# SyncE waits for the first maximum row of the second quad before it issues the next image's query copies

## What is computed

```python
h = group_norm(x, groups=32) * gamma + beta
q, k, v = split(einsum('oc,bct->bot', qkv_w, h) + qkv_b)      # per head, 16 channels
w = softmax(einsum('bct,bcs->bts', q * s, k * s))             # 1024 x 1024 per head, s = 16 ** -0.25
a = einsum('bts,bcs->bct', w, v)
x = x + einsum('oc,bct->bot', proj_w, a) + proj_b
```

## Time and profile before

| | us |
|---|---|
| median of 3 runs | 2296.9 |
| lowest and highest run | 2295.36, 2297.52 |
| span of the profiled execution | 2295.6 |
| PE busy | 2201.2 (96%) |
| DVE busy | 1815.8 (79%) |
| ACT busy | 1719.9 (75%) |
| eight-head part, up to | about 1714 |

### The profile page before, as it was taken

The page is one execution under the profiler, slowest core; times in us unless marked ns, Lnnn a source line. Parts: engine busy times, 40 slices in busy tenths (PEclk is TensorE's granted clock), DMA queues, the critical chain, the costliest instruction groups (busy, mean ns, idle before and its releaser), DMA issues. The chain is left out here.

```text
span 2295.6 us, 34006 instructions
## 1 busy us (share of the span) xinstructions
PE 2201.2 (96%) x11776; PEld 972.2 (42%) x11776; DVE 1815.8 (79%) x3176; ACT 1719.9 (75%) x3107; POOL 520.6 (23%) x689
## 2 busy tenths in 40 slices
PE   3999999999999999999999999999989999999998
PEld 1223232323333232333333232333326888888887
DVE  2878888888888878888888888888837777777776
ACT  1467677777877777776767777776777888888887
POOL 3113030202213030311203020211113333333331
PEclk9999999999999999999999999999999999999999
DMA  6053351606244261616345160615112112121111
GB/s 82 7 70 53 58 78 35 104 22 91 41 69 66 45 90 36 95 27 84 50 61 76 36 103 22 94 37 75 26 31 72 53 48 66 36 65 57 42 53 49
DMA packets 81647, 132.31 MB, mean 58 GB/s; under 512 B 17632, under 2 KB 50528, under 8 KB 81504
## 3 DMA queue, kind: packets, MB, share of 16 engines
q1 hardware_dynamic: 78240, 129.70, 32.5%
q10 hardware_dynamic: 3264, 0.79, 0.2%
HBM read 53.12 MB, written 17.83 MB: 31 GB/s over the span
## 5 line engine op out<-in xcount | busy, mean ns | idle before, releaser
L447 DVE TENSOR_REDUCE h_half_nmax<-h_s_ps 128x1 f32<-128x512 f32 x2048 | 1285.8, 684 | 270.2 <-PE h_s_ps L682 263.0
L598 ACT ACTIVATE h_probs<-h_st_ps 128x512 f32<-128x512 f32 x2048 | 1103.7, 600 | 388.2 <-PE h_st_ps L819 382.2
L682 PE MATMUL h_s_ps<-h_krep,h_qrep 96*128 96x512 bf16 x2048 | 795.7, 389 | 22.4 <-SPq L232 20.8
L819 PE MATMUL h_st_ps<-h_qrep,h_krep 99*128 99x512 bf16 x2048 | 779.9, 382 | 35.1 <-DMA h_qrep<-h_mrow 24.3
L674 PE MATMUL h_pv<-h_probs,h_vT 128*32 128x512 f32 x4096 | 548.1, 607 | 0.9 <-ACT h_probs L598 0.7
L682 PEld LDWEIGHTS h_s_ps<-h_krep,h_qrep 96*128 96x128 bf16 x2048 | 200.0, 98 | 677.3 <-DVE h_half_nmax L447 503.0
L819 PEld LDWEIGHTS h_st_ps<-h_qrep,h_krep 99*128 99x128 bf16 x2048 | 201.7, 99 | 230.6 <-DMA h_qrep<-h_mrow 36.4
L347 POOL TENSOR_SCALAR h_nparts<-h_nmax 128x16 bf16<-128x16 f32 x64 | 16.4, 256 | 956.6 <-DVE h_nmax L455 956.6
L1334 PE MATMUL o_s<-o_k,o_q 128*128 128x512 f32 x768 | 225.7, 430 | 7.4 <-DVE o_q L1155 5.8
L1334 PE MATMUL o_pv<-o_pT,o_vT 128*128 128x512 f32 x768 | 208.1, 406 | 0.8 <-ACTq L1261 0.8
L1149 DVE TENSOR_TENSOR o_pT<-o_t,o_pT 128x512 fp32r<-128x512 f32 x256 | 164.5, 684 | 43.8 <-ACT o_pT L1286 41.4
(11 more groups left out here) (116 smaller groups left out, 1380.1 us busy)
## 6 DMA issues: line engine op xcount, KB each, us to landing
h_krep<-h_kp SPq DMA_DIRECT2D x96, 256.0 KB, 8.7
h_qrep<-h_qp SPq DMA_DIRECT2D x192, 128.0 KB, 9.5
x_res<-out_dram SPq DMA_DIRECT2D x24, 512.0 KB, 3.7
num<-av SPq DMA_DIRECT2D x128, 64.0 KB
rrep<-rden_dram SPq DMA_DIRECT2D x16, 512.0 KB
out_dram<-o_y SPq DMA_DIRECT2D x16, 512.0 KB
out_dram<-h_y SPq DMA_DIRECT2D x15, 512.0 KB, 2.6
o_x_in<-out_dram SPq DMA_DIRECT2D x15, 512.0 KB, 3.5
```

The costliest lines, as they stand in the source:

```text
L447: reduce = nc.vector.tensor_reduce(half_nmax[:, c, unit:unit + 1], s_ps[bank(2 * n + c)][:, :], AX.X, ALU.max, negate=True)
L598: nc.scalar.activation(probs[g % 2][:, j, :], st_ps[bank(n)][:, :], ACT.Exp, scale=1.0 / CH ** 0.5).then_inc(exp_done, 1)
L682: nc.tensor.matmul(s_ps[bank(n)][:, :], qrep[par][0:KS, th, head, tile * P:(tile + 1) * P], krep[par][0:KS, head, c * HALF:(c + 1) * HALF] ...
L819: nc.tensor.matmul(st_ps[bank(n)][:, :], krep[par][0:KM, head, st * P:(st + 1) * P], qrep[par][0:KM, th, head, :], start=True, stop=True). ...
```

## The change

`replicate` gets a third argument, `rows`. Where it is given, SP waits, after the query parts are ready and before the query copies, until `mrow_dma` has counted that many rows. In the body it is given as `4 * u + 3`: the third row of that image's count, which is the one of the second quad's first half. The copies at the start of the program pass nothing. No DMA is added or removed, and PE's program is unchanged.

```diff
-            def replicate(par, u):
+            def replicate(par, u, rows=None):
 
                 sp.wait_ge(parts_ready, 2 * u + 1)
                 for term, part in enumerate((0, 1, 2, 0, 1, 0)):
                     sp.dma_start(krep[par][term * CH:(term + 1) * CH, :, :], parts["k"][:, part, :]).then_inc(rep_dma, 16)
                 sp.wait_ge(parts_ready, 2 * u + 2)
+                if rows is not None:
+                    sp.wait_ge(mrow_dma, 16 * rows)
                 for term, part in enumerate((0, 0, 0, 1, 1, 2)):
                     for th in range(2):
                         sp.dma_start(qrep[par][term * CH:(term + 1) * CH, th, :, :],
...
                     if not (last and u == 1):
-                        replicate(1 - u, u)
+                        replicate(1 - u, u, 4 * u + 3)
```

## The result

The changed kernel takes 2267.9 us (median of 4 runs, 2266.39 to 2268.76) beside 2297.2 for the kernel before on the same chip: ratio 0.9875, 95% interval 0.9862 to 0.9887, 29.3 us faster. The forecast was 2279.5, from 2269 to 2291. The profiled span fell from 2295.6 to 2265.9.

A forecast was written before the change was run, and what follows sets the result against it. PE was taken as the bound, held up by a row standing behind query copies. Gain 31.0 less 13.6 of new waits is 17.4 us; span 2295.6 becomes 2278.2, with the median 1.3 above: 2279.5, range 2269 to 2291.

The forecast's parts named there:

- What the row's lateness cost, 31.0: PE's waits on the maximum row at quad hand-overs, with lowered clock behind two: 31.0 us, all gained by the change.
- m: The start of the maximum row's DMA issue by ACT, from which the prediction counts times in us.
- SP's start, m + 2.4: SP, after waiting for the row's landing, issues the query copies from about m + 2.4; bounds 1.9 and 3.3.
- The copies, 16.9 from issue to matmul: Query copies: first bytes 1.3, transfer 14.1 at 111 GB/s, landing to PE's matmul 1.5; sum 16.9 us.
- The new wait, 0.8 an image: PE waits 0.8 us for the query copies in each of 14 ordinary images, 11.2 us together.
- The first image, 2.4: Without output projections, PE wants the first image's copies at m + 16.94 and waits 2.4 us; no clock loss counted.
- SP's later work, free: Store of y, four loads and gather, queued on SP behind the copies, start later but cost nothing; cover 5.0 us.
- the copies land in time: Rival: copies need 16.1 us or less, so ordinary images have no new wait; 30.9 us gained, 2266.0, chance 0.12.

The follow-up runs named there:

- the run with the first copies alone: Changed kernel, but at the program's start SP waits for the six key copies to land before issuing the twelve query copies; 2270.5 us, one run.
- the thirteenth copy: Changed kernel plus one 128 KB copy to a spare buffer behind the twelve query copies, waited for with them; 2285.1 us, ratio 0.9942.
- the delay: Changed kernel plus a 12 KB DMA issued and waited for between the row's landing and the query copies, some 2.3 us; 2325.8 us, ratio 1.0123.
- the run that waits for the keys: Changed kernel, but SP waits for the landing of the six key copies instead of for the row; 2285.6 us, ratio 0.9952.

## Why the forecast missed, step by step

- **What the row's lateness cost, 31.0: held.** The waits on the row are gone, L821 starts at m + 6.83, and neither hand-over loses the clock. Counted from the rows, 31.0 less what is left of new waits (1.9, below) is 29.1; the spans differ by 29.7. The last transposed score tile of the eight-head layers moved from 1713.4 to 1684.9, 28.5; the rest of the 29.7 lies in the one-head layers, which the change doesn't touch. Counted image by image in the trace before, the first row score comes 30.8 us later in sum than it does with six copies ahead; the first image's part of that is 5.5, where the prediction had 2.89 + 2.88.
- **SP's start, m + 2.4: m + 2.28.** Within the bounds, 0.1 off.
- **The copies, 16.9 from issue to matmul: 16.1. This is the step that failed.** Its parts: first bytes 1.2 for 1.3, bytes 13.4 for 14.1, landing and wake-up some 1.5 as taken. The 14.1 came from 111 GB/s, read where query copies run behind keys; on empty queues they move at 117 on the mean, which the run with the first copies alone shows to be due to the queues. The gain is in their first two us (167 GB/s); for the rest they run at 112, about as forecast. The 118 of the third image would have given 13.3, but it is a stretch behind the keys too, and right by luck.
- **The new wait, 0.8 an image: none.** With 0.1 and 0.8 us less, the copies are there at m + 18.4 to 18.5 in most images, and PE wants them at m + 18.50. That takes away the 11.2 us of fourteen waits. In four images the row score is still 0.06 to 0.27 us late, 0.7 in all, too little for the view of the waits. That lateness is paid in full is right: the thirteenth copy and the delay show it.
- **The first image, 2.4: 1.1.** L821 comes earlier than in an ordinary image because the output projections are left out, as forecast. But the copies are wanted at m + 17.24 and not at 16.94 (L821 at m + 5.12, and from there to the row score 12.12 as with six copies ahead, not 11.67), and they come at m + 18.38 and not at 19.3. No loss of clock, as taken. 11.2 - 0.7 in the ordinary images and 2.4 - 1.1 here make 11.8, which accounts for the 11.6 us by which the forecast missed.
- **SP's later work, free: held.** The gather follows at 358.96 = m + 25.7 (m + 27.9 was reckoned), L396 starts at m + 32.1, and the next row's L821 at 363.19 doesn't wait.
- **The rivals.** What came is "the copies land in time", given 0.12, with its own limit of 16.1 met to a tenth. Its 2266.0 belongs to copies of 14.6 us; at the limit of 16.1 the first image would wait 2.4 + 16.1 - 16.94 = 1.6, and the time is 2296.9 - 31.0 + 1.6 = 2267.5, beside the measured 2267.9. That they came 0.1 us early, and not late, is luck: nothing in the change sees to it. The range was cut at 2269 although the bound of 14.6 us belonged to this case: fourteen images multiply a term of 16 us that was uncertain by 1, so 0.7 us made 10 us, and the two sides of the edge are not alike. Early gives nothing more, late costs 15 us for each microsecond.

## What to carry to other kernels

In this kernel a small urgent DMA waits for the large ones that were issued ahead of it, even from another engine's queue; if it has a deadline, issue it first, and hold back only as many of the large ones as would still be queued at that moment. Holding back all of them puts their own deadline at risk: here the kernel ended within 0.1 us of a cliff that costs 15 us a microsecond, while six of twelve copies ahead of the row, or a wait for the row's issue instead of its landing, keep the gain with 7.2 and 1.5 us to spare in the ordinary images. Six ahead took another 1.9 us on one chip. When a forecast hangs on a transfer being in time, read its duration where the queues stand as they will stand, its first two us apart from the rest, and put the edge, not the middle, into the range.

## What the runs showed that was not expected

- Query copies issued ahead of the row held it up across the two DMA queues. With twelve and nine of them ahead, L821 started 8.14 and 8.04 after the row's issue; with six, which were through by then, 6.83 (no wait); and with copies issued 0.87 us behind it, it wasn't late. The Trainium skill, page "DMA: Bandwidth & Descriptors", section "Queues, rings and completion order", has each DMA engine alternate between the queues that have work; by that the row would have passed the copies that still waited ahead of it, and no run here shows it do so. Why they held it is open.
- Waits of PE of 2.2 us cost more than themselves: in the run with the delay the clock fell to 1.2 GHz behind six of fifteen, where the 1.1 us waits of the thirteenth copy left the time at one for one (only its longest, the first image's of 2.2, lowered the clock). The length of a wait alone doesn't tell: in the run with the delay one of 2.01 (the eighth image) lowered the clock and one of 2.38 (the ninth) did not, nor did the 2.47 of the run that waits for the keys.
- Query copies move at 117 GB/s on the mean when they start on empty queues and at 110 behind key copies, 13.4 us beside 14.3. Most of the difference is in their first two us, 167 GB/s beside 115. Why the beginning is quicker is open.
